# The feed-forward part of a fused cross-attention and mixture kernel: a tile every two steps instead of every three, inside one round

## The reference, cut to what matters

```
x = x + mlstm(layernorm(x), ctx, ctx, gates, rpe, ln_w, ln_b, hops)      # attention
xf = layernorm(x)
weights, selected = top_k(softmax(xf @ gate_w.T), 2)                     # router
z = einsum('td,erd->ter', xf, lora_A)
moe = einsum('ter,te,eor->to', z, ew, lora_B) * 2                        # ew: normalised weights
x = x + xf @ base_w.T + base_b + moe
```

## Time and profile before

| | |
|---|---|
| time, median of 3 runs | 3701.87 us (3699.72 to 3703.38) |
| the profiled execution | 3707.81 us |
| its span, first to last instruction | 3706.1 us |
| busy in the span | PE 3237.0, DVE 2667.8, POOL 2031.3, ACT 1768.3 us |
| mean granted TensorE clock | 0.944 of full speed |

### The profile page before, as it was taken

The page is one execution under the profiler, slowest core; times in us unless marked ns, Lnnn a source line. Parts: engine busy times, 40 slices in busy tenths (PEclk is TensorE's granted clock), DMA queues, the critical chain, the costliest instruction groups (busy, mean ns, idle before and its releaser), DMA issues.

```text
span 3706.1 us, 70399 instructions
## 1 busy us (share of the span) xinstructions
PE 3237.0 (87%) x24884; PEld 1904.7 (51%) x24884; DVE 2667.8 (72%) x5497; ACT 1768.3 (48%) x4225; POOL 2031.3 (55%) x2248
## 2 busy tenths in 40 slices
PE   5777777777777777699999999999999999999997
PEld 4454454544445444355555555555555555555554
DVE  5455555555555555588888889888888898888885
ACT  2444444444444444455555555555555555555552
POOL 5677777777777776244444444444444444444443
PEclk8888888898998899799999999999999999999999
DMA  8999999999999998655555555555555555555541
GB/s 254 315 315 316 318 318 316 317 320 317 333 322 327 325 323 287 190 151 169 160 152 173 152 170 157 155 168 161 156 169 156 166 157 156 167 161 158 166 141 50
DMA packets 409680, 814.16 MB, mean 220 GB/s; under 512 B 100314, under 2 KB 204762, under 8 KB 407284
## 3 DMA queue, kind: packets, MB, share of 16 engines
q1 hardware_dynamic: 303860, 453.05, 39.7%
q0 software_dynamic: 87040, 285.28, 23.5%
q10 hardware_dynamic: 18432, 71.31, 5.1%
HBM read 632.67 MB, written 176.69 MB: 218 GB/s over the span
## 4 chain that ended last, share of the span: by engine, by line
PE 58%; DMA 15%; POOL 9%; DVE 9%; issue 6%; ACT 3%; SPq 0%; DVEq 0%; ACTq 0%
DMA arena<-in_L_xattn_rpe_dram,arena 15%; PE psum L1406 12%; PE psum L1349 7%; PE psum L1357 7%; PE psum L1269 7%; PE psum L1373 7%; POOL arena L683 7%; PE psum L1296 6%; PE psum L1285 3%; PE psum L1327 3%; PE psum L1408 3%; PE psum L1424 3%; POOL arena L674 2%; DVE arena L1179 1%; DVE arena L1073 1%
## 5 line engine op out<-in xcount | busy, mean ns | idle before, releaser
L1269 PE MATMUL psum<-arena 128*128 128x128 f32 x4352 | 691.5, 309 | 254.6 <-DMA arena<-in_L_xattn_rpe_dram,arena 237.5
L683 POOL DMA_INDIRECT arena<-in_L_xattn_rpe_dram,arena x768 | 728.7, 949 | 270.9 <-issue 181.8
L1269 PEld LDWEIGHTS psum<-arena 128*128 128x128 f32 x4352 | 545.3, 157 | 516.3 <-DMA arena<-in_L_xattn_rpe_dram,arena 357.7
L702 POOL TENSOR_SCALAR_AFFINE_SELECT arena<-arena 128x256 f32<-128x256 f32 x256 | 105.2, 411 | 746.9 <-ACT arena L826 644.4
L1406 PE MATMUL psum<-arena 128*128 128x512 f32 x1024 | 489.9, 608 | 22.0 <-ACT arena L806 22.0
L826 ACT ACTIVATE arena<-arena 128x512 f32<-128x512 f32 (+3 forms) x1024 | 503.4, 559 | 6.1 <-DMA arena<-gate_rows 5.3
L513 DVE COPY arena<-psum 128x512 f32<-128x512 f32 x384 | 263.3, 688 | 303.4 <-PE psum L1269 299.5
L1073 DVE TENSOR_TENSOR arena<-psum,arena 128x1024 f32<-128x1024 f32 (+1 forms) x384 | 397.5, 1041 | 37.6 <-PE psum L1357 31.1
L522 DVE COPY arena<-psum 128x416 f32<-128x416 f32 (+15 forms) x512 | 224.7, 441 | 266.8 <-PE psum L1285 261.1
L1285 PE MATMUL psum<-arena 64*32 64x416 f32 (+7 forms) x8192 | 370.6, 431 | 30.1 <-ACT arena L750 15.9
L674 POOL DMA_INDIRECT arena<-in_L_xattn_rpe_dram,arena x320 | 304.3, 951 | 165.0 <-issue 75.9
(11 more groups left out here) (104 smaller groups left out, 4772.4 us busy)
## 6 DMA issues: line engine op xcount, KB each, us to landing
arena<-in_x_dram SPq DMA_DIRECT2D x256, 256.0 KB, 3.3
arena<-gate_rows SPq DMA_DIRECT2D x128, 512.0 KB, 4.6
arena<-in_x_dram SPq DMA_DIRECT2D x512, 64.0 KB
arena<-in_ctx_dram SPq DMA_DIRECT2D x32, 1024.0 KB, 7.7
out_dram<-arena SPq DMA_DIRECT2D x128, 256.0 KB, 2.3
arena<-in_L_xattn_rpe_dram,arena POOLq DMA_INDIRECT x1088
arena<-hop_products SPq DMA_DIRECT2D x128, 128.0 KB, 2.6
arena<-hop_products SPq DMA_DIRECT2D x128, 120.0 KB, 2.6
```

Source lines behind the costliest of these rows:

```text
L683: nc.gpsimd.indirect_dma_start(out=rows[v][:, t, :], out_offset=None, in_=rpe[:, :], in_offset=bass.IndirectOffsetOnAxis(ap=here[:, t, v:v ...
L1269: last = nc.tensor.transpose(turn_bank(o)[:, q * P:(q + 1) * P], own[:, q * P:(q + 1) * P], ident)
```

## The change

- The tables of the feed-forward part: tile `t` begins at step 1 + 2t. Entries now reach from 1 to 12; only `OUT` of tile 3 falls into the next round (its step 0). `TwoRounds.start` leaves out a part that has no steps.
- On TensorE `base` now stands ahead of the feed-forward transposes of the same step, and the first of those waits also for the first context copy.
- The first context tile is turned into bank 7, not 6; its waits and those of the second change with it, and the later ones lose waits that are no longer needed.
- ScalarE's `queries(0)` moves from behind the router's Exp to behind the head root of the same step.
- VectorE's `OUT` in step 0 stands behind that step's mul, not at the head of the step.
- `gate_stats` transposes only the 40 rows that are used (four transposes of 40 x 128).
- The waits of `base`, `gates` and `gate_stats` on other readers of bank 6 follow the new steps.

```diff
-        C_TURN, C_BANK = [0, 1, 2, 3], [6, 6, 5, 5]
+        C_TURN, C_BANK = [0, 1, 2, 3], [7, 6, 5, 5]
...
-        SCALE = [1, 4, 7, 10]
-        LAYER = [2, 5, 8, 11]
-        TURN = [3, 6, 9, 12]
-        ROUTE = [4, 7, 10, 13]
-        BASE = [5, 8, 11, 14]
-        OUT = [6, 9, 12, 15]
+        SCALE = [1, 3, 5, 7]
+        LAYER = [2, 4, 6, 8]
+        TURN = [3, 5, 7, 9]
+        ROUTE = [4, 6, 8, 10]
+        BASE = [5, 7, 9, 11]
+        OUT = [6, 8, 10, 12]
...
+                    if rp and s == X_TURN[0]:
+                        queries(0)
                     if rp and s == LOG:
...
-                    for t in at_step(X_TURN, s):
-                        if rp and not t:
-                            queries(t)
...
                     for t, r in due(OUT, s, rf, rg):
-                        output(r, t)
+                        if s:
+                            output(r, t)
...
                     if ra:
                         unit_weights(s)
+                    for t, r in due(OUT, s, rf, rg):
+                        if not s:
+                            output(r, t)
...
                     if rf:
-                        pe.wait_ge(*dve_f.at(rf.b, ("out", 1)))
-                    turn(6, g_rows).then_inc(pe_p.sem, pe_p.step("stats"))
+                        pe.wait_ge(*dve_f.at(rf.b, ("out", 2)))
+                    for k in range(KT):
+                        last = nc.tensor.transpose(bank(6)[:, k * P:k * P + GR], g_rows[0:GR, k * P:(k + 1) * P],
+                                                   ident[0:GR, 0:GR])
+                    last.then_inc(pe_p.sem, pe_p.step("stats"))
...
-                        read = (("x", 3), "gctx", "stats", ("x", 0))[t]
+                        read = (("x", 3), "gctx", "gctx", "stats")[t]
...
+                    for t, r in due(BASE, s, rf, rg):
+                        base(r, t)
                     for t, r in due(TURN, s, rf, rg):
                         pe.wait_ge(*dve_f.at(r.b, ("norm", t)))
 
                         if t:
                             pe.wait_ge(*act_f.at(r.b, ("mixT", t - 1)))
-                        elif rg:
-                            pe.wait_ge(*act_f.at(rg.b, ("mixT", ST - 1)))
+                        else:
+                            if rg:
+                                pe.wait_ge(*act_f.at(rg.b, ("mixT", ST - 1)))
+                            if rp:
+                                pe.wait_ge(act_p.sem, act_p.done(rp.b, ("c", 0)))
                         turn(7, ffn_x).then_inc(*pe_f.inc(("turn", t)))
-                    for t, r in due(BASE, s, rf, rg):
-                        base(r, t)
```

More of the change, by code:

```diff
@@ L80, in start @@
     def start(self, engine):
-        self.early.start(engine)
-        self.late.start(engine)
+        for part in (self.early, self.late):
+            if part.n:
+                part.start(engine)
     def at(self, rnd, name, back=0):
@@ L432, in build @@
                 act_f_steps[part].append(("mixT", t))
+            for t in at_step(BASE, s):
+                pe_f_steps[part].append(("base", t))
             for t in at_step(TURN, s):
@@ L435, in build @@
                 act_f_steps[part].append(("xT", t))
-            for t in at_step(BASE, s):
-                pe_f_steps[part].append(("base", t))
         dve_f = TwoRounds(*(Stage(sem(f"dve_f{i}"), dve_f_steps[i]) for i in range(2)))
@@ L1302, in turn_context @@
                         pe.wait_ge(ctx_loaded, rp.b * 16 + 16)
+                        if rg:
+                            pe.wait_ge(*act_f.at(rg.b, ("mixT", ST - 1)))
+                    elif t == 1:
                         pe.wait_ge(act_p.sem, act_p.done(rp.b, "stats", 1))
                         if rg:
-                            pe.wait_ge(*dve_f.at(rg.b, ("out", 2)))
+                            pe.wait_ge(*dve_f.at(rg.b, ("out", ST - 1)))
                     else:
-                        pe.wait_ge(act_p.sem, act_p.done(rp.b, ("c", t - 1)))
+                        if t == 3:
+                            pe.wait_ge(act_p.sem, act_p.done(rp.b, ("c", t - 1)))
                         if t == 2 and rf:
@@ L1314, in turn_queries @@
                     pe.wait_ge(act_p.sem, act_p.done(rp.b, ("x", t - 1) if t else ("c", 1)))
-                    if t == 1 and rg:
-                        pe.wait_ge(*dve_f.at(rg.b, ("out", 3)))
                     turn(6, xq_norm[t % 2]).then_inc(pe_p.sem, pe_p.step(("x", t)))
```

## The result

The changed kernel takes **3868.99 us**, the median of 4 runs (3862.61 to 3869.97), beside 3700.8 us for the kernel before on the same chip: a ratio of **1.0451** (95% interval 1.0438 to 1.0464), 4.5% slower. The unaltered changed kernel was run once more in a later comparison: 3865.58 us, 1.0451 [1.0434, 1.0469]. The profiled execution took 3869.06 us.

A forecast was written before the change was run, and what follows sets the result against it. TensorE bounds the full rounds, with 66.5 us of work and 0.76 of waiting. Moved work +3.2, clock +1.1 and steps 8 to 10 +0.7 make +4.95 a round, +144 over 29; the ends cancel: 3846 us, range 3755 to 3905.

The forecast's parts named there:

- both waits: Full rounds: TensorE waits for the norm (2 to 3 us) and for mul 1 (1 to 1.5 us).
- The cover: turn(3), route(3) and base(3), 6.1 us of TensorE work leaving steps 0 to 2, covered a chain on other engines.
- Rival 1: The cover in steps 0 to 2 isn't needed, so the kernel gets faster: 3666 us; chance 0.08.
- The chain: From scores(0) to the feed-forward turn(0): 17.5 us in the changed kernel, against 20.23 before.
- The clock: Behind the norm's stall TensorE's clock drops to 1.2 GHz, counted at two thirds: +1.1 us a round.
- Steps 8 to 10: VectorE runs late and TensorE waits for OUT(2) at the gate statistics: +0.7 us a round, between 0 and 2.5.
- The statistics: Gate statistics' four transposes, cut to 40 rows, save 0.2 us a round, between 0 and 0.25.
- The work: TensorE's own work in a full round: 66.5 us before the change, less 0.2 for the statistics.
- The ends: Outside the full rounds: first rf round +5.9, round without rp about +3, tail -8, lead-in -1 us.
- Rivals 3 and 4: 3: stalls without clock drop, 3795 or 3752 us, below range 0.04; 4: VectorE jams in second half, 3914 us, above 0.05.

The follow-up runs named there:

- GpSimd waits: The changed kernel, with GpSimd's x_b of tile 1 waiting for VectorE's norm of tile 0: 3804.61 us, ratio 1.0276.
- filler: The changed kernel with twenty useless transposes of 128 columns ahead of the feed-forward turn(0) in step 3: 3807.86 us, ratio 1.0288.
- both: The changed kernel with twenty useless transposes ahead of turn(0) and GpSimd's x_b of tile 1 waiting for the norm of tile 0: 3762.28 us.
- tile 3 back: The changed kernel with tile 3 alone on its old steps and the first context tile back in bank 6: 3731.95 us, ratio 1.008.
- tile 3 back, GpSimd waits: The changed kernel with tile 3 on its old steps and GpSimd's x_b of tile 1 waiting for the norm of tile 0: 3697.06 us.

## Why the prediction came out right, and where its steps were off

The forecast was 3846 us with 3755 to 3905; the direction, both waits, their places and the fall of the clock were as forecast. The size of the norm's wait wasn't: 3.95 us, where the prediction had named 2 to 3; mul 1 held TensorE 1.07 us, of the 1 to 1.5 named. That the time came within 23 us is in part luck: terms too small by 1.8 us a round met terms too large by 1.2.

The rounds of all kernels add up from three parts. TensorE's work in a round is 69.62 - 3.79 = 65.8 us, from the rounds of the kernel with GpSimd's wait in which the clock stayed up. So the first row is no test of it, and in the last row the clock's term is what is left over; the four between are tests.

| kernel | work + filler | waits | lower clock | sum | measured round |
|---|---|---|---|---|---|
| GpSimd waits | 65.8 | 2.74 + 1.06 | 1.63 x 21/27 | 70.9 | 70.93 |
| filler | 65.8 + 2.4 | 1.64 + 1.06 | 0.1 | 71.0 | 70.94 |
| both | 65.8 + 2.4 | 0.42 + 1.07 | 0 | 69.7 | 69.67 |
| tile 3 back | 65.8 | 1.05 + 0.83 + 0.52 | 0 | 68.2 | 68.31 |
| tile 3 back, GpSimd waits | 65.8 | 0.83 + 0.52 | 0 | 67.2 | 67.19 |
| changed | 65.8 | 3.95 + 1.07 | 2.0 (the rest) | | 72.83 |

Point by point, against the sum of 72.2 us:

- **The cover.** The step on which all rested, that the 6.1 us moved out of steps 0 to 2 were cover, held: with tile 3 back, 137 us return. Rival 1 is refuted by the waits of 5.0 us in every round.
- **The chain**, 17.5 us from `scores(0)` to `turn(0)`: 18.58. This is the term that was mis-sized. I took the chain of the first `rf` round, in which the norm takes 0.54 us (VectorE's L1179 at 1588.82 us), and didn't ask what GpSimd does beside it once tile 1 comes a step earlier. It costs 1.2 us: with GpSimd waiting the chain is 17.4 (1635.63 to 1653.01 us), as forecast. The waits are 5.0 in place of the 4.1 in my sum, +0.9.
- **The clock**: +1.1 forecast, about 2.0 measured. I had taken it for two thirds of the rounds, from stalls of 2.40 to 3.2 us. Behind the longer wait it fell in every round, and in a third of them it stayed down for longer (4.81 us in such a one and 4.06 in another, against the 4.16 of the earlier trace rows). With a wait of the forecast kind, 2.74 us, it fell in 21 of 27 rounds.
- **Steps 8 to 10**: +0.7 forecast, 0 measured. VectorE does wait in step 8, as forecast, 3.02 us for `base(1)`. But its router took 2.8 us there, not the 3.7 I had taken. The 3.2 us of the earlier trace rows weren't of a quiet stretch: in that router L1142 takes 0.80 us (2590.43 us), in this one 0.14 (2568.28). And `OUT(2)` was there in time, by some 0.1 us only, so that this term at 0 is luck as well (first fence VectorE, second TensorE):

```profile
2565.31 0.69 DVE L1124 TENSOR_TENSOR arena<-psum,arena 128x512 f32<-128x512 f32 x1 [3.02 <-PE psum L1417]
...
2578.80 0.67 DVE L1124 TENSOR_TENSOR arena<-psum,arena 128x512 f32<-128x512 f32 x1
```

```profile
2579.61 0.41 PE L1343 MATMUL psum<-arena 40*128 40x40 f32 x4
2579.95 1.08 PE L1382 MATMUL psum<-arena 128*64 128x512 f32 x4
```

- **The statistics**: 0.2 forecast. The four transposes take 0.34 us from start to start, against 0.52, so 0.18. By the Trainium skill (TensorE: Matmul & The Clock Gate, "LDWEIGHTS") the prediction had an estimate of 0.43 for four; the measurement decides.
- **The work**: 65.8, against 66.3 in my sum (66.5 less the 0.2), -0.5. Of this 0.3 is in the last two passes of `base` (3.52 us a round from start to start, 3.80 before), 0.1 in the overlap of a matmul's modelled end with the next one's start, which a wait swallows; 0.1 is open.
- **The ends**: first `rf` round +7.3 (forecast +5.9), round without `rp` +1.9 (+3), tail -6.7 (-8), lead-in -2.5 (-1). Their sum is 0, as forecast, but with a lead-in that varies by 8 us from one execution to the next this is luck. In the tail tiles follow each other in 8.5 to 8.7 us once the first is through, against 9.67.

+0.9 +0.9 -0.7 -0.5 is +0.6 a round, 17.4 us in 29 rounds; the rounds' 161.2 less the forecast's 144 is 17.2. The rest of the 22.99 us between 3846 and 3868.99 is the execution shown of before, 6 us above its median, with which I had scaled. Rivals 3 and 4 had the pieces the wrong way round: the clock fell in every round, and the second half did not jam.

## What to carry to other kernels

Before work is moved ahead in a pipeline, ask what it covered where it stood: an engine that is busy all the time may still be filling the gap of a chain on other engines, and that chain's length, not the work, then sets the round. The cheapest place to read that length is a round at the pipeline's end in which the work is missing, but what else moves beside the chain (here GpSimd's addition beside the norm) must be added. And put GpSimd's additions beside VectorE's operations that aren't stretched by them, here a multiplication with one input in PSUM: that took away the last wait, which moving VectorE's work to other steps, or the addition behind the sixth of the head variance's eight operations, had not.

## What the runs showed of the hardware

- A VectorE operation of 0.2 us on 32 columns takes 1.2 us when it starts 0.11 to 0.13 us after the start of a GpSimd addition of 512 columns (1.27 us), and ends 0.04 to 0.05 us after the addition's end. Which of the eight is hit depends only on which one starts next after the addition. A norm of 0.54 us takes up to 1.54 beside such work, and ends 0.28 to 0.29 us after it. A mul with an input in PSUM (1.21 us), statistics (0.68) and reductions (0.67) aren't hit.
- How long TensorE had idled and what the granted clock was behind it: behind 3.95 us it fell in 27 of 27 rounds, behind 2.74 us in 21 of 27, behind 1.64 us in 1 of 27, behind 1.05 us in none of 28. Useless transposes in the wait (2.4 us of it) kept it up in 26 of 27 rounds, and the kernel was 61 us faster, though it did more work.
- The part ahead of the full rounds varies by 8 us between two executions of the same kernel, more than some of the edits are worth.
